# Graph pooling by gathered rows: the GpSimd queue paced by what VectorE has taken instead of by landed rows

## The reference

```
h   = input @ weight
out = maximum(adj @ h + bias, 0)                          # 4096 x 128
# graph pool: for each node the elementwise maximum of `out` over its neighbours
masked = where(adj_blk[:, :, None] != 0, out[None, :, :], neg)
pooled = max(masked, axis=1)
```

## The kernel before

| rows of | taken at blocks |
|---|---|
| tile 0 | 11 to 13 |
| tile 1 | 17 to 19 |
| longer lists (`overflow_maxima`, L1934 and L1938) | 23 and 24 |
| tile 2 | 27 to 29 |
| tile 3 | 3 to 5 of the group after |

## Time and profile before

### The profile page before, as it was taken

The page is one execution under the profiler, slowest core; times in us unless marked ns, Lnnn a source line. Parts: engine busy times, 40 slices in busy tenths (PEclk is TensorE's granted clock), DMA queues, the critical chain, the costliest instruction groups (busy, mean ns, idle before and its releaser), DMA issues.

```text
span 1753.8 us, 31129 instructions
## 1 busy us (share of the span) xinstructions
PE 1538.2 (88%) x8740; PEld 920.7 (52%) x8740; DVE 1257.8 (72%) x3409; ACT 767.4 (44%) x1175; POOL 631.2 (36%) x822
## 2 busy tenths in 40 slices
PE   4999999865887888798969999999999999858997
PEld 3777777522333333576745666777444444424554
DVE  7799999964777777648856666632899999923434
ACT  3444444323555545358742223765565565500000
POOL 5333333356555556534510001333000000165664
PEclk8999999977999999899989999999999999978999
DMA  8688787523323223333303223443000000033442
GB/s 287 222 306 302 277 292 293 184 67 109 85 80 78 78 77 85 95 110 102 96 13 120 84 89 109 126 124 117 0 0 12 6 6 6 19 108 119 138 133 78
DMA packets 160459, 202.99 MB, mean 116 GB/s; under 512 B 11940, under 2 KB 133730, under 8 KB 152208
## 3 DMA queue, kind: packets, MB, share of 16 engines
q1 hardware_dynamic: 136000, 174.68, 30.0%
q0 software_dynamic: 11728, 21.33, 4.7%
q10 hardware_dynamic: 12672, 6.29, 1.2%
HBM read 178.85 MB, written 28.38 MB: 118 GB/s over the span
## 4 chain that ended last, share of the span: by engine, by line
PE 55%; DVE 17%; issue 16%; POOL 4%; DMA 3%; ACT 3%; DVEq 1%; POOLq 0%; ACTq 0%; SPq 0%
PE bank L707 19%; PE bank L773 9%; PE bank L585 8%; DVE partsA L2294 5%; PE bank L627 5%; PE bank L882 4%; POOL gath L1456 3%; PE bank L590 3%; PE bank L561 2%; DMA gath<-pool_features,idx_now 2%; PE bank L614 2%; DVE cand L1767 2%; PE bank L548 1%; DVE hn L1680 1%; PE bank L883 1%
## 5 line engine op out<-in xcount | busy, mean ns | idle before, releaser
L707 PE MATMUL bank<-partsB,panel 128*128 128x387 bf16 (+1 forms) x2048 | 368.2, 338 | 56.4 <-issue 34.3
L707 PEld LDWEIGHTS bank<-partsB,panel 128*128 128x128 fp8e4 x2048 | 204.5, 100 | 215.9 <-issue 74.8
L882 PE MATMUL bank<-wide,partsA 128*128 128x512 f32 x512 | 263.2, 596 | 6.3 <-ACT rows L1253 4.9
L1767 DVE MAX8 cand<-bank 128x8 f32<-128x128 f32 x1024 | 217.7, 292 | 10.4 <-PE bank L590 6.4
L984 ACT ACTIVATE first<-bank 128x512 fp8e4<-128x512 f32 x256 | 139.2, 596 | 196.1 <-PE bank L614 116.4
L627 PE MATMUL bank<-first,partsB 128*128 128x512 fp8e4 x768 | 202.7, 403 | 19.9 <-issue 17.3
L585 PE MATMUL bank<-partsA,panel 128*128 128x387 bf16 x1024 | 212.0, 329 | 6.4 <-DVE cand L1767 5.3
L1900 DVE TENSOR_TENSOR gath<-gath,bank 128x512 f32<-128x512 f32 x240 | 161.3, 683 | 76.6 <-remote 49.2
L1456 POOL DMA_INDIRECT gath<-pool_features,idx_now x160 | 171.1, 1069 | 109.3 <-DMA gath<-pool_features,idx_now 43.2
L773 PE MATMUL bank<-adj_ring,layer_halves 128*128 128x512 f32 x768 | 198.4, 409 | 8.8 <-POOL adj_ring L1520 5.4
L937 ACT ACTIVATE panel<-bank 128x1024 fp8e4<-128x1024 bf16 x128 | 131.1, 1025 | 146.4 <-PE bank L561 146.4
(11 more groups left out here) (281 smaller groups left out, 2147.1 us busy)
## 6 DMA issues: line engine op xcount, KB each, us to landing
rows<-in_adj SPq DMA_DIRECT2D x64, 1024.0 KB, 7.2
panel<-adjT_panels SPq DMA_DIRECT2D x192, 256.0 KB
panel<-adjT_panels SPq DMA_DIRECT2D x64, 512.0 KB
adjT_panels<-panel SPq DMA_DIRECT2D x32, 512.0 KB, 3.0
gath<-pool_features,idx_now POOLq DMA_INDIRECT x160
overflow_maxima<-wide POOLq DMA_DIRECT2D x1, 2048.0 KB, 21.0
tail_maxima<-wide POOLq DMA_DIRECT2D x1, 2048.0 KB, 25.7
pool_features<-gsc ACTq DMA_DIRECT2D x8, 256.0 KB, 2.3
```

The costliest lines, as they stand in the source:

```text
L707: i = pe.matmul(bank[q][:, 0:3 * w], panel[:, q, j, :], of_block if w < FE else parts_of[u][:, j, :], start=(j == 0), stop=(j == NT - 1))
L882: pe.matmul(o[:, :], zs[:, q % 2, :], zT[:, c * 512:(c + 1) * 512], start=True, stop=False)
L1767: i = dve.max(cand[:, ch * BPB + b, :], bank[4 + ch % 4][:, b * P:(b + 1) * P])
```

## The change

The waits of the GpSimd queue on landed rows go (`rows_landed`, and the wait on `s_over_gath`). In their place the queue waits five times a group for VectorE's count of block pairs: tile 0's gathers for the last pair of the group before (not in group 0), tile 1's for pair 3 (blocks 6 and 7), the longer lists' for pair 6 (12 and 13), tile 2's for pair 8 (16 and 17), tile 3's for pair 11 (22 and 23). VectorE's own waits on the landed rows stay, and so does everything else.

```diff
+TURN_OF_TILE = (None, 3, 8, 11)
+TURN_OF_LONGER = 6
...
-            def rows_landed(g, q):
-
-                pool.wait_ge(s_gath[q], 16 * MAIN * (g + 1))
-
-            def gathers(g, q):
+            def pair_taken(g, pair):
+
+                pool.wait_ge(s_fp_used, HT * g + pair + 1 + 2)
+
+            def gathers(g, q, first):
                 t = g * G + q
                 pool.wait_ge(s_idx, t + 1)
                 pool.wait_ge(s_main_clear, t + 1)
-                if q in (1, 3):
-                    rows_landed(g, q - 1)
+                if q:
+                    pair_taken(g, TURN_OF_TILE[q])
+                elif not first:
+                    pair_taken(g - 1, HT - 1)
...
                 pool.wait_ge(s_over_clear, g + 1)
+                pair_taken(g, TURN_OF_LONGER)
...
                 for k in range(MAIN, MAIN + MIDDLE):
                     gather_overflow(k)
-                pool.wait_ge(s_over_gath, 16 * MIDDLE * (g + 1))
...
             def turn(g, peeled):
                 for q in range(G):
-                    gathers(g, q)
+                    gathers(g, q, peeled)
                     if q == 1:
-                        rows_landed(g, q)
                         overflow_gathers(g)
```

## The result

The changed kernel took 1763.55 us in the median of 20 runs (1755.74 to 1788.78), the kernel before 1752.14 us in 20 runs beside it (1744.0 to 1757.58). The ratio is 1.008, with a 95% interval of 1.0058 to 1.0102; it leaves out the one slow run, of 1788.78 us. That is slower by 0.8%, small but clear of the noise, where 17 us of gain were forecast. The profiled execution has a span of 1759.2 us, against 1753.8.

The account below looks back on a forecast made before the run. GpSimd's queue, with its landing waits, was taken to bound the pool stage. Tile waits of 16.2 us and 0.9 in group 0 would go, 17.1 together, from 1755.5 to 1738.4: 1738 for the median, range 1705 to 1753.

Parts of the forecast that it names:

- The bound: Pool stage: GpSimd's queue sets the period, 43.1 us a group, of which 10.8 are landing waits.
- The restart of the queue: GpSimd idle before a tile's gathers, waiting for VectorE's pair count: 0.9 us a tile, range 0 to 0.9.
- What does not go: VectorE's idle time in groups 2 to 7: 8.1 us a group stay, mostly remote block waits at blocks 4 to 8.
- the sum: Pool stage gains: 12 us in groups 2 to 7, 3.1 after group 7, 2.0 in group 0, together 17.1.
- rival 3: Pool stage: gathers without a pause stall blocks a second time each group, 42 us less 17: 1780; chance 0.13.
- rival 2: Pool stage: more block waits or a late tile 2 give back 8 to 25 us: 1746 to 1764; chance 0.14.
- Rival 1: Block waits at each group's start shrink too: half gone 1719, chance 0.2; all gone 1700, chance 0.07.
- The loop through both engines: VectorE and GpSimd from block 13 round to block 13: 38.6 us in group 3, 32.7 without two block waits.
- The rule against the change: GpSimd can't write descriptors while VectorE holds the shared port: 9 us more a group, which ends the gain.
- The order of the rows: Gathered rows reach VectorE in time in each group; only tile 2 is near its limit, waiting 0 to 1 us.

Follow-up runs that it names:

- chip 2: Changed kernel and kernel before rerun there with no edit: 1654.64 against 1700.82 us, ratio 0.972; changed kernel without any pace: 1650.70 us.
- chip 8: Kernel before less its landing wait between longer lists and tile 2: 1683.22 us, ratio 0.9898; changed kernel without pair waits: 1651.07 us against 1698.7.
- chip 11: Against the kernel before (1697.63 us): changed kernel 1656.76, changed kernel with landing waits back before tiles 2 and 3 1675.02, without any pace 1650.60.
- chips 2, 3 and 11: Changed kernel rerun with no edit against the kernel before on three chips: 1654.64, 1654.66 and 1656.76 us, ratios 0.972, 0.9725 and 0.9749.
- The stand-in: Selection products of blocks 16 to 29 done twice, on another chip: kernel before with it 1706.98 us, changed kernel with it 1703.70.

## Why the prediction was wrong

**The bound was read rightly.** GpSimd's queue set the period through its landing waits, and removing them removes VectorE's waits for rows: 24.1 us of waits went in the first pair of profiles, where 17.1 net were forecast, 52.5 on chip 2. One of the four taken out alone (chip 8) is worth 15.5 us, two put back into the changed kernel cost 18 (chip 11). The restart of the queue, put at 0.9 us, is 0.87 to 0.89 in groups 2 to 7 of both profiles of the changed kernel (measured pair and chip 2).

**The step that failed is "What does not go".** It took the 8.1 us a group of block waits for a fixed cost in a fixed place ("I cost this at no change"), tied to SyncE's work after the store. They grew from 71.5 to 109.4 us, and moved: from blocks 2 to 6 in most groups before (the prediction read 4 to 8) to blocks 22 to 28 in most now. In the terms of the sum: 12 us of gain were forecast for groups 2 to 7 and 13.4 of loss came, 2.0 of gain for group 0 and 7.0 of loss came by the end of group 1; behind group 7 the gain was 9.0 and not 3.1. The late signals now begin ahead of the store and thus of SyncE's work behind it: in group 4 of the changed kernel VectorE's late starts are at 585.34 and 591.06, and the store comes after both, in GpSimd's timeline:

```profile
593.99 1.03 POOL L1501 DMA_INDIRECT overflow_maxima<-gath,rest  x1 [0.30 <-issue]
```

SyncE's load of the stored maxima follows at 596.60, and between 581.80 and 592.55 it issues nothing at all. So a backlog behind that load is not their cause. In both profiles most of them lie where gathers have run on without a pause (11 DMAs to 515.6 before; 19 from 568.9 to 595.0 now, with one copy among them), which is rival 3's description, given 13% and 1780 us; the time itself lies at the upper end of rival 2's, 1764.

**But rival 3's cause is not the whole one.** The row of gathers alone doesn't delay a signal: chips 2, 3 and 11 run rows of up to 24 with the pair waits, and without pace one of 94 (chips 8 and 11), with none late. Late signals need something of the chip or its surroundings as well, which no run here could switch on. With it, both kernels are slow. TensorE's late updates are about as many in both (50 and 54 of those recorded), but more of them reach VectorE in the changed kernel: laid pair by pair beside TensorE's ends, VectorE starts over 0.5 us late in 25 of the 128 pairs, where it was 16, and stands idle for 75.1 us by it, where it was 52.5. On chip 2 it is none in either kernel. The account of the spans, measured pair minus chip 2: kernel before 1753.8 - 1696.8 = 57.0, of which groups 2 to 7 only 251.9 - 249.0 = 2.9. Changed kernel 1759.2 - 1655.2 = 104.0, of which groups 2 to 7 are 265.3 - 215.0 = 50.3 and groups 0 and 1 another 13.8. Most of what is left is the last stage, which the change doesn't touch: GpSimd's gathers of nearest rows, L1573, first to last start. The kernel before where the change was measured, then on chip 2:

```profile
L1573 POOL DMA_INDIRECT gath<-last_features,IDX x128: 941/947/1413, 1535.9 to 1738.4; - x128
```

```profile
L1573 POOL DMA_INDIRECT gath<-last_features,IDX x128: 939/944/1441, 1525.8 to 1687.2; - x128
```

202.5 against 161.4 us; in the changed kernel it is 196.4 against 161.3. VectorE's largest waits in that stage are, in the same order:

```profile
DVE agg L1703 <- remote: 70.3, 12, 13.9
```

```profile
DVE agg L2367 <- DMA gath<-last_features,IDX: 75.4, 28, 4.6
```

So late signals show in the two stages in which GpSimd issues indirect gathers, and not between them; the search of the top rows, which lies in between and has no gathers, takes the same time to 0.1 us on both:

```profile
L2294 DVE MAX8 partsA<-rows x28: 4407/4410/4428, 1239.3 to 1486.3; 128x8 f32<-128x4096 f32 x28
```

```profile
L2294 DVE MAX8 partsA<-rows x28: 4406/4409/4429, 1229.3 to 1476.3; 128x8 f32<-128x4096 f32 x28
```

**What is shown and what is argued.** Shown: the changed kernel gains 41 to 46 us where signals are on time (chips 2, 3 and 11, ratios 0.972 to 0.975), and there a longer TensorE takes nearly all of that gain away, so that both kernels come to nearly the same time. Shown in the one pair of profiles: TensorE's signals come late in both kernels, and VectorE loses 22.6 us more by them in the changed one. Argued from these: that this is why the measured result is 1.008. The stand-in ends level, 1703.7 against 1707.0, and not slower; it explains the lost gain and not the last 0.8%. Open: what makes signals late, whether the products or only the word of them is late, whether the chip or the moment decides, and whether in that condition the length of the row of gathers does, as the places suggest. The kernel with two landing waits back was to tell the last; it only ran where nothing is late.

**Rival 1** (block waits shrink) is what happened on the experiments' chips: 26.4 us in the changed kernel, none remote; but its range began at 1700 because it was counted from 1755. The loop through both engines without block waits was put at 32.7 us a group; 34.8 was measured. **The rule against the change** (VectorE's lock on the shared port, in the Trainium skill's "SBUF — State Buffer", section "SBUF: two separate sides") does not show in this case's traces: the median gather is 997 ns in the changed kernel on chip 2, with VectorE busy for 31.3 of 34.8 us. **The order of the rows** was right in kind: where signals are on time, tile 2 is the latest in groups 2 to 7 (under 0.6 us a time), and all waits for tile rows are 4.6 us in seven, the longest 1.4, in group 0.

A version without any pace is the fastest wherever signals are on time: 1651 us against 1655 and 1701 on chip 2, 1651 against 1657 and 1698 on chip 11. The five pair waits are worth nothing there, and cost 4 to 6 us; staged indices and cleared slots hold the queue enough.

## What to carry to other kernels

A queue that idles for its own landings hides delays elsewhere; take the waits out and those delays come to light, so ask of each remaining wait what it would cost with no cover, and put the same delay into both kernels to see (the same products cost 8 us in the one and 49 in the other). Don't count a wait whose releaser the profile can't name as a constant: lay the producer's end beside the consumer's start (0.11 us here, or 6.0), and look whether the place moves. And measure a change of queue pacing on more than one chip, and more than once, before you believe its sign: 1.008 and 0.972 are the same edit.

## What the runs showed of the hardware

- TensorE's semaphore updates can come late, by 4.7 and 5.9 us for the two pairs shown and by up to 11.0 in the stage, in both profiles of the measured pair, and there only in the stages with GpSimd's indirect gathers. The gathers themselves are no slower then (median 997 and 1000 ns), and the updates of VectorE and ScalarE are on time (within 0.01 us). In the pool stage of the 14 profiles of the experiments none is over 0.02 us late, and VectorE starts some 0.1 us after TensorE's end.
- The granted clock of TensorE is lower where it waits: in the measured profile 0.89 of full speed over windows of 45 to 47 us, with waits of 4 us at a time; in the changed kernel on chip 2 it is 1.00 in five windows of 35 us in a row.
- A gather with an index for each of 128 rows costs GpSimd 1.30 us from start to start; on chip 2 the changed kernel's tile gathers landed 2.3 to 3.5 us after their start, with a median of 2.5. After a wait for VectorE's count the first gather starts 0.87 to 0.89 us after VectorE's last maximum.
